# Transposing the attention probabilities by block moves and VectorE, a new order of the loop, and a new start of the kernel

## The chip, the cores and the metric

The kernel runs on one core of one Trainium2 chip. The metric is the device time of one execution in microseconds (us), the median of several executions of the whole program, with inputs and outputs in the chip's main memory.

## The reference

The input x has 8 sequences of 1024 rows of 512 numbers. An attention layer with a memory, and then a feed-forward layer, each followed by a residual sum and a layer norm:

```
q, k, v = x @ Wq, x @ Wk, x @ Wv            # 8 heads of 64, in segments of 128 rows
per head and segment, in order of segments:
    sq, sk  = elu(q) + 1, elu(k) + 1
    att_mem = sq @ mem / (sq @ z)
    mem, z  = mem + sk^T @ v, z + sum(sk)
    att_dot = softmax(q @ k^T / 8) @ v
    att     = gate * att_mem + (1 - gate) * att_dot      # gate = sigmoid(betas)
x = layernorm(x + concat(att) @ Wo)
W1q, W2q = each weight as -1, 0 or 1, after division by the mean of |W|
x = layernorm(x + relu(x @ W1q^T + b1) @ W2q^T + b2)     # 512 -> 2048 -> 512
```

Everything is float32.

## The kernel before

The program is written engine by engine, and every engine runs its own list, held in step by semaphores. The work is cut into 32 groups of two sequences by one segment (2 x 128 rows); two groups are live in the memory `mem`, so a group reads what the group two before it wrote. The main loop of each engine runs over g and does in iteration g a piece of group g (attention), of group g-1 and of group g-2 (feed-forward), in an order written out by hand.

Float32 products are made of float16 halves: an operand is split into a high half (ScalarE writes it) and a low half (VectorE or GpSimd subtracts), and TensorE adds three products (two where the weight is -1, 0 or 1). TensorE needs its operands with the summed index on the partitions, so x, the attention result, the normed rows and the probabilities have to be transposed. Three of these (`x_blocks`, `att_dot`, `y_blocks`), and `sk_t`, go by **moved blocks**: SyncE issues 16 DMAs (8 for x) that carry 32x32 blocks to their transposed places in runs of 128 bytes, and a VectorE instruction then turns each block where it lies. The probabilities go by TensorE: `turn_p` (L289) multiplies each 128x128 matrix by an identity, 16 matrices per group, into a PSUM bank, from which ScalarE (`p_split`, L1059) and VectorE (`p_split`, L660) write `pt_hi` and `pt_lo`.

TensorE's jobs of attention take turns in four PSUM banks (`take`, L214), each waiting until the bank's last reader is done. `ffn_up` (L366, eight pieces of a group, j = 0 to 7, 16 matmuls each) uses two banks more: piece j waits for the relu of piece j-2 (`h_relu`, L1086, ScalarE). `ffn_down` (L383, four pieces for each of the two sequences, 8 matmuls each) has a bank for each sequence, and needs the halves of h from `h_split` (VectorE, L771; pieces with an even j also their low half) and `h_rest` (GpSimd, L1303; the low half of those with an odd j). In iteration g, TensorE runs pieces 5 to 7 of `ffn_up` and all of `ffn_down` for group g-2, and pieces 0 to 4 of `ffn_up` for group g-1.

SyncE's list in an iteration is: blocks of x for g+1, `bounce_out` (the row maxima of x to main memory, from where `bounce_back` reads them to all partitions to find the scale of x), `move_y(g-1)`, `bounce_back`, `move_sk(g)`, `put_out(g-2)` (L1492), `move_att(g)`, and rows of x for g+2. A queue issues in order, so a step that waits holds what stands behind it. `load_x` (L1385) waits for the output that lay in the same rows.

Iteration 0 also prepares the weights: `w_max`, `w_split` and so on for the four attention weights, and for W1 and W2 the sums (`w_sum`), thresholds, 32 blocks of comparisons (`compare`, by VectorE and GpSimd), their transposes (`turn_w`) and copies (`put_w`). The gates' 512 values are spread to all partitions through main memory (`gates_out`, `gates_back`, L1434), in runs of 16 bytes. GpSimd multiplies by them in `gate_mix` (L1234).

The order in which `prob` comes to the matmuls:

```
def turn_p(g, t, half):                     # TensorE, bank from take()
    pe.wait_ge(sem["pexp"], by_half(g, t, half))
    for i in range(4):
        ins = pe.transpose(ps[:, i], prob[:, t, 4 * half + i], ident32[:])
```

Of the kernel before, what the change touches and what calls it, by code (L numbers as in the profile page):

```python
# [5 lines left out]
ALU = mybir.AluOpType  # L6
ACT = mybir.ActivationFunctionType
F32 = mybir.dt.float32
# [23 lines left out]
    xblocks ablocks yblocks skblocks xturn xt_hi xt kproj qproj kq_exp klo qlo elu vproj v_hi v1 v  # L32
    score rowmax exp_bias pexp pturn pt_hi pt skturn
    reset_fill reset mem num den attm invsum mix pv attd gated mixed upd
# [5 lines left out]
def build_program(nc, x, Wq, Wk, Wv, betas, Wo, W1, b1, W2, b2, out):  # L40
# [14 lines left out]
    with ctx:  # L55
# [33 lines left out]
        y_blocks = sb("y_blocks", [P, TG, D])  # L89
# [14 lines left out]
        pt_hi = sb("pt_hi", [P, TG, H, P], F16)  # L104
        pt_lo = sb("pt_lo", [P, TG, H, P], F16)
# [4 lines left out]
        at = sb("at", [P, TG, 2 * KT, P], F16)  # L110
# [10 lines left out]
        gate_dram = nc.dram_tensor("gate_dram", [P, 3, D // P], F32, kind="Internal").ap()  # L121
# [9 lines left out]
        h32 = flat[:, 4096:4096 + NH32 * 512].rearrange("p (b t) -> p b t", b=NH32)  # L131
        yt = sb("yt", [P, 2, TG, 2 * KT, P], F16)
# [42 lines left out]

        def two_pairs(rows_of, j):
            return rows_of[:, :, 2 * j:2 * j + 2].rearrange("p t c n -> p t (c n)")
# [28 lines left out]

        block = ctx.enter_context(nc.Block())

        @block.tensor
        def _(pe):  # L210
# [3 lines left out]
            def take(job):  # L214
# [6 lines left out]
                return b  # L221

# [32 lines left out]
            def project_v(g, t):  # L255
# [3 lines left out]
                if g == 0:  # L259
                    pe.wait_ge(sem["wsplit_pool"], 2)  # L260
# [27 lines left out]

            def turn_p(g, t, half):  # L289
                if not 0 <= g < NG:  # L290
                    return
                b = take(("p", g, t, half))
                ps = banks[b][:].rearrange("p (h t) -> p h t", h=4)
                pe.wait_ge(sem["pexp"], by_half(g, t, half))
                for i in range(4):
                    ins = pe.transpose(ps[:, i], prob[:, t, 4 * half + i], ident32[:])  # L296
                ins.then_inc(sem["pturn"], 1)
                bank_free[b] = (sem["pt"], by_half(g, t, half))
# [53 lines left out]
            def project_out(g, t):  # L352
# [3 lines left out]
                if g == 0 and t == 0:  # L356
                    pe.wait_ge(sem["wsplit_pool"], 4)
# [89 lines left out]
            spread_amax()  # L447
            turn_max(0)
            spread_max(0)
            for g in range(NG + 2):  # L450
                project_qk(g, "k", 0)
                if g == 0:
                    turn_max(1)
                    spread_max(1)
                    turn_max(2)
                    spread_max(2)
                ffn_up(g - 2, 5)
                project_qk(g, "k", 1)
                project_qk(g, "q", 0)
                ffn_up(g - 2, 6)  # L460
                project_qk(g, "q", 1)
# [1094 lines left out]
```

## Time and profile before

| what | value |
|---|---|
| median of 3 runs | 1965.37 us (1965.0 to 1965.46) |
| the profiled execution's own time | 1962.89 us |
| its span | 1961.1 us |
| granted TensorE clock, mean over the span | 0.982 of full speed |
| TensorE, matmuls busy | 1862.8 us |
| VectorE busy | 1488.7 us |
| ScalarE busy | 1003.6 us |
| GpSimd busy | 813.9 us |
| DMA | 619144 packets, 121.20 MB, of them 592800 packets under 512 B |

The span is the time from the first to the last instruction of the profiled execution; its own time is 1.79 us longer, and the median of the runs 2.48 us longer than that. An engine's busy time counts its instructions and not the issue of DMAs: what ScalarE's or SyncE's queue spends on those stands in the timeline of the queue. A matmul's record is longer than what the next one waits for; the distance between starts is the price of one.

### The profile page before, as it was taken

Reading aid. Unit: us, or ns where it says so; the run is one execution under the profiler, and the core shown is the slowest. Engines: PE = TensorE matmul, PEld = TensorE weight load, DVE = VectorE, ACT = ScalarE, POOL = GpSimd, SP = SyncE. Lnnn points to the kernel's source line nnn. Section 1 sums busy time; section 2 is a strip of 40 time slices with the busy share of each in tenths; the row PEclk is TensorE's granted clock in tenths of the full one; section 3 lists DMA queues with packets and bytes.
Section 4 is the critical chain, followed back from the end, with each engine's and each line's share of the span. In section 5 each row is a group of like instructions: output and inputs, shape, how many; then the busy total and the mean of one; then the engine's idle time right before and its main releaser. Section 6 shows DMA issues by size and latency. Waiting matters only on the chain.

```text
span 1961.1 us, 44984 instructions
## 1 busy us (share of the span) xinstructions
PE 1862.8 (95%) x16663; PEld 1312.6 (67%) x16663; DVE 1488.7 (76%) x2991; ACT 1003.6 (51%) x2426; POOL 813.9 (42%) x810
## 2 busy tenths in 40 slices
PE   3478999999999999999999999999999999999987
PEld 2266666777766677776667777666677776667754
DVE  4577877777887777778877777887777788777763
ACT  2655555455555555554555555455545555555531
POOL 0563443344444334444443444444334444433443
PEclk9688999999999999999999999999999999999999
DMA  7932233333323333332323233223332332323121
GB/s 226 105 74 50 47 55 57 60 59 65 64 45 61 53 58 61 63 67 45 60 52 63 58 60 67 54 53 56 57 59 58 66 63 47 61 50 62 37 39 33
DMA packets 619144, 121.20 MB, mean 62 GB/s; under 512 B 592800, under 2 KB 596784, under 8 KB 618416
## 3 DMA queue, kind: packets, MB, share of 16 engines
q1 hardware_dynamic: 616640, 114.11, 30.9%
q10 hardware_dynamic: 2288, 4.20, 0.6%
q8 instruction: 135, 2.21, 0.5%
q14 instruction: 81, 0.66, 0.2%
HBM read 51.06 MB, written 16.80 MB: 35 GB/s over the span
## 4 chain that ended last, share of the span: by engine, by line
PE 91%; DVE 3%; issue 2%; SPq 2%; ACT 1%; POOL 1%; DMA 0%; POOLq 0%; DVEq 0%; ACTq 0%
PE bank L393 11%; PE bank L379 11%; PE bank L380 11%; PE bank L394 11%; PE bank L249 6%; PE bank L251 6%; PE bank L250 6%; PE bank L317 3%; PE bank L263 3%; PE bank L296 3%; PE bank L360 3%; PE bank L265 3%; PE bank L361 3%; PE bank L264 3%; PE bank L362 3%
## 5 line engine op out<-in xcount | busy, mean ns | idle before, releaser
L379 PE MATMUL bank<-yt,w1t 128*128 128x256 f16 x2048 | 456.9, 273 | 2.9 <-POOL yt L1278 2.9
L380 PE MATMUL bank<-yt,w1t 128*128 128x256 f16 x2048 | 456.5, 273 | 0.0
L1101 ACT ACTIVATE arena<-bank,b_scaled,wscalars 128x256 f32<-128x256 f32 x512 | 261.4, 562 | 379.4 <-PE bank L380 291.5
L393 PE MATMUL bank<-w2t,arena 128*128 128x512 f16 x1024 | 388.7, 380 | 2.1 <-POOL arena L1310 2.1
L394 PE MATMUL bank<-w2t,arena 128*128 128x512 f16 x1024 | 388.1, 379 | 0.0
L1055 ACT ACTIVATE prob<-bank,exp_bias,gscalars 128x128 f32<-128x128 f32 x512 | 227.2, 459 | 229.8 <-DVE exp_bias L657 228.6
L1310 POOL TENSOR_TENSOR arena<-arena 128x512 f16<-128x512 f32 x128 | 172.0, 1344 | 270.3 <-DVE arena L780 270.3
L1271 POOL TENSOR_TENSOR at<-att_dot,at 128x512 f16<-128x512 f32 x64 | 74.1, 1159 | 416.7 <-ACT at L1074 416.7
L379 PEld LDWEIGHTS bank<-yt,w1t 128*128 128x128 f16 x2048 | 200.7, 98 | 28.4 <-issue 3.4
L380 PEld LDWEIGHTS bank<-yt,w1t 128*128 128x128 f16 x2048 | 200.7, 98 | 22.6
L393 PEld LDWEIGHTS bank<-w2t,arena 128*128 128x128 f16 x1024 | 100.0, 98 | 113.6 <-issue 3.1
L1243 POOL TENSOR_TENSOR att_mem<-att_mem,gate_in 128x512 f32<-128x512 f32 x64 | 81.7, 1276 | 220.3 <-DVE att_mem L696 197.1
L394 PEld LDWEIGHTS bank<-w2t,arena 128*128 128x128 f16 x1024 | 100.2, 98 | 106.7
L620 DVE SCALAR_TENSOR_TENSOR k_lo<-bank,k_hi 128x512 f16<-128x512 f32 x64 | 44.2, 691 | 139.2 <-ACT relu_tmp L1028 139.2
L249 PE MATMUL bank<-xt,wk_hi 128*128 128x256 f16 x512 | 141.1, 276 | 6.3 <-DVE wk_lo L812 6.0
L780 DVE CAST arena<-arena 128x512 f16<-128x512 f32 x256 | 139.0, 553 | 7.7 <-ACT arena L1101 7.5
L783 DVE TENSOR_TENSOR arena<-arena 128x512 f16<-128x512 f32 x128 | 140.4, 1097 | 4.4
L250 PE MATMUL bank<-xt,wk_hi 128*128 128x256 f16 x512 | 141.0, 275 | 0.0
L251 PE MATMUL bank<-xt,wk_lo 128*128 128x256 f16 x512 | 141.0, 275 | 0.0
L251 PE MATMUL bank<-xt,wq_lo 128*128 128x256 f16 x512 | 139.6, 273 | 0.0
L249 PE MATMUL bank<-xt,wq_hi 128*128 128x256 f16 x512 | 139.6, 273 | 0.0
L250 PE MATMUL bank<-xt,wq_hi 128*128 128x256 f16 x512 | 139.6, 273 | 0.0
(177 smaller groups left out, 4464.2 us busy)
## 6 DMA issues: line engine op xcount, KB each, us to landing
x_blocks<-in_L_attn_x SPq DMA_DIRECT2D x256, 64.0 KB, 2.9
rows<-in_L_attn_x SPq DMA_DIRECT2D x32, 512.0 KB, 3.9
sk<-sk_t SPq DMA_DIRECT2D x512, 32.0 KB, 2.0
att_dot<-att_mem SPq DMA_DIRECT2D x512, 32.0 KB, 2.0
y_blocks<-rows SPq DMA_DIRECT2D x512, 32.0 KB
out_rows<-rows SPq DMA_DIRECT2D x64, 256.0 KB, 2.0
arena<-in_L_ffn_W SPq DMA_DIRECT2D x6, 1024.0 KB, 5.8
w2t<-in_L_ffn_W SPq DMA_DIRECT2D x2, 1024.0 KB, 9.6
```

What stands on the lines that cost most here:

```text
L249: pe.matmul(ps[:, :, c], w_hi[n][:, k, cols], xt[:, :, k], start=k == 0, stop=False)
L250: pe.matmul(ps[:, :, c], w_hi[n][:, k, cols], xt[:, :, KT + k], start=False, stop=False)
L251: ins = pe.matmul(ps[:, :, c], w_lo[n][:, k, cols], xt[:, :, k], start=False, stop=k == KT - 1)
L379: pe.matmul(ps[:, c], w1t[:, k, cols], yt[:, g % 2, :, k], start=k == 0, stop=False)
L380: ins = pe.matmul(ps[:, c], w1t[:, k, cols], yt[:, g % 2, :, KT + k], start=False, stop=k == KT - 1)
L393: pe.matmul(banks[own][:], h_hi[:, f, toks], w2t[:, f, :], start=f == 0, stop=False)
L394: ins = pe.matmul(banks[own][:], h_lo[:, f, toks], w2t[:, f, :], start=False, stop=f == FT - 1)
L780: dve.tensor_copy(hi, h32[:, n % NH32]).then_inc(sem["h_hi"], 1)
L783: dve.tensor_tensor(lo, h32[:, n % NH32], hi, ALU.subtract).then_inc(sem["h_dve"], 1)
L1055: ins = act.activation(prob[:, t, at], ps[:, c], ACT.Exp, scale=gcol(g, G_EXP), bias=exp_bias[:, t, at:at + 1], accum_out=row_sum[:, t, h: ...
L1101: ins = act.activation(h32[:, n % NH32, c * GT:(c + 1) * GT], ps[:, c], ACT.Relu, scale=w(H_SCALE_Y), bias=b1_scaled[:, f:f + 1])
L1310: pool.tensor_tensor(lo, h32[:, n % NH32], hi, ALU.subtract).then_inc(sem["h_pool"], 1)
```

## The change

1. **The probabilities.** TensorE's `turn_p` goes. Once all exponentials of a group are there, ScalarE's queue issues 16 DMAs (`move_p`) of 64 KB, that carry 32x32 blocks of `prob` to `p_blocks`; VectorE turns the blocks (two instructions of 128x1024 per group), and the two `p_split` read `p_blocks` in SBUF in place of PSUM banks. `pt_hi` and `pt_lo` now lie over `prob`, so the exponentials of a group wait for `pv` of the group before.
2. **The order of the loop.** All engines' lists are written anew. The whole feed-forward of a group (eight pieces up, eight down) is now in one iteration, g-2; `update_memory` is done one iteration later. On SyncE `bounce_back` follows `bounce_out` at once, `move_att(g)` stands before `put_out(g-2)`, and `load_x` right behind that.
3. **The start.** Group 0 is not loaded as blocks: its rows are the first DMA, the maximum is taken of them, and TensorE transposes them (8 transposes). All weight loads go through SyncE, k, q, v first. Low halves of Wv are VectorE's in place of GpSimd's. The gates are written to main memory so that they are read back in runs of 2 KB.

The core of the diff (the engines' loops are shown for TensorE; the others are rewritten in the same way):

```diff
+        def move_blocks(engine, dst, src, done):
+
+            for b in range(4):
+                for a in range(4):
+                    engine.dma_start(dst[32 * a:32 * a + 32, :, :, 32 * b:32 * b + 32],
+                                     src[32 * b:32 * b + 32, :, :, 32 * a:32 * a + 32]).then_inc(done, 16)
...
-                    act.wait_ge(sem["pturn"], by_half(g - 1, t, half))
+                    act.wait_ge(sem["pv"], by_t(g - 1, t))
...
+            def move_p(g):
+                act.wait_ge(sem["pexp"], by_half(g, 1, 1))
+                if g:
+                    act.wait_ge(sem["pt"], by_half(g - 1, 1, 1))
+                move_blocks(act, p_blocks, prob, sem["pblocks"])
...
+            def turn_p(g, t):
+                flat_p = p_blocks[:, t].rearrange("p h c -> p (h c)")
+                dve.wait_ge(sem["pblocks"], MOVED * (g + 1))
+                dve.transpose(flat_p, flat_p).then_inc(sem["pturn"], 1)
...
-                pool.wait_ge(sem["gated"], 2 * by_t(g, t))
+                pool.wait_ge(sem["gated_in"], by_t(g, t))
+                pool.wait_ge(sem["gated"], by_t(g, t))
...
-                    sp.dma_start(gate[:].rearrange("p (n q) -> p n q", q=D // P),
-                                 gate_dram[:, i].partition_broadcast(P)).then_inc(sem["gates"], 16)
+                    sp.dma_start(gate[:], gate_dram[i].rearrange("p n -> (p n)").partition_broadcast(P)).then_inc(sem["gates"], 16)
```

TensorE's list of an iteration, without what only g = 0 has. Before:

```
k 0 | up(g-2,5) | k 1, q 0 | up(g-2,6) | q 1 | up(g-2,7) | out(g-1, 0 and 1) | scores 0 | v 0
| down(g-2, 0: 0, 1) | turn_p | v 1 | down(g-2, 0: 2) | scores 1 | read 0 | down(g-2, 0: 3; 1: 0) | turn_p
| down(g-2, 1: 1) | turn_p x2 | attend 0 | down(g-2, 1: 2) | read 1 | down(g-2, 1: 3) | attend 1
| up(g-1, 0 to 3) | update(g, 0 and 1) | up(g-1, 4)
```

After:

```
k 0, k 1, q 0, q 1 | up(g-2, 0, 1) | update(g-1, 0) | read 0 | scores 0 | up(g-2, 2, 3) | scores 1
| update(g-1, 1) | up(g-2, 4) | out(g-1, 0 and 1) | up(g-2, 5) | v 0 | read 1 | up(g-2, 6)
| down(g-2, 0: 0) | v 1 | up(g-2, 7) | down(g-2, 0: 1, 2, 3; 1: 0) | attend 0 | down(g-2, 1: 1)
| attend 1 | down(g-2, 1: 2, 3)
```

**ScalarE, a middle group, from the exponentials to the split of the probabilities.** The tile `arena` holds h (the relu of `ffn_up`). Before:

```order
L1055 ACTIVATE prob,row_sum<-bank,exp_bias,gscalars 128x128 x4
L1041 ACTIVATE v_hi<-bank 128x512
L1042 ACTIVATE v<-bank,gscalars 128x8x64
L1055 ACTIVATE prob,row_sum<-bank,exp_bias,gscalars 128x128 x4
L1066 ACTIVATE pt_hi<-bank 128x512
L1041 ACTIVATE v_hi<-bank 128x512
L1042 ACTIVATE v<-bank,gscalars 128x8x64
L1055 ACTIVATE prob,row_sum<-bank,exp_bias,gscalars 128x128 x8
L1066 ACTIVATE pt_hi<-bank 128x512 x2
```

With the change:

```order
L1080 ACTIVATE prob,row_sum<-bank,exp_bias,gscalars 128x128 x4
L1132 ACTIVATE arena<-bank,b_scaled,wscalars 128x256 x2
L1080 ACTIVATE prob,row_sum<-bank,exp_bias,gscalars 128x128 x4
L1132 ACTIVATE arena<-bank,b_scaled,wscalars 128x256 x2
L1080 ACTIVATE prob,row_sum<-bank,exp_bias,gscalars 128x128 x8
L1132 ACTIVATE arena<-bank,b_scaled,wscalars 128x256 x2
L217 DMA p_blocks<-prob 32x16x32 x16
L1132 ACTIVATE arena<-bank,b_scaled,wscalars 128x256 x4
L1066 ACTIVATE v_hi<-bank 128x512
L1067 ACTIVATE v<-bank,gscalars 128x8x64
L1132 ACTIVATE arena<-bank,b_scaled,wscalars 128x256 x2
L1097 ACTIVATE prob<-p_blocks 128x512 x4
```

The relus of pieces 2, 3 and 4 now stand between the exponentials, and those of pieces 5, 6 and 7, the split of v and all four `p_split` stand behind the 16 DMAs.

**SyncE, one iteration in the middle of the program.** Before:

```order
L1408 DMA x_blocks<-in_L_attn_x 32x16x32 x8
L1449 DMA amax_dram<-amax 128x1
L1464 DMA y_blocks<-rows 32x8x32 x16
L1456 DMA amax_row<-amax_dram 128x128
L1476 DMA sk<-sk_t 32x8x32 x16
L1497 DMA out_rows<-rows 128x512 x2
L1464 DMA att_dot<-att_mem 32x8x32 x16
L1395 DMA rows<-in_L_attn_x 128x2x512
```

With the change:

```order
L1430 DMA x_blocks<-in_L_attn_x 32x16x32 x8
L1473 DMA amax_dram<-amax 128x1
L1480 DMA amax_row<-amax_dram 128x128
L217 DMA y_blocks<-rows 32x8x32 x16
L217 DMA sk<-sk_t 32x8x32 x16
L217 DMA att_dot<-att_mem 32x8x32 x16
L1509 DMA out_rows<-rows 128x512 x2
L1417 DMA rows<-in_L_attn_x 128x2x512
```

The read back of the maxima stands right behind their write, ahead of the blocks of y, and the output right ahead of the load into the rows it frees.

## Rows read from the trace of the kernel before

**Rows 1.** The page: busy time of each engine, and the chain that ended last
```profile
PE 1862.8 (95%) x16663; PEld 1312.6 (67%) x16663; DVE 1488.7 (76%) x2991; ACT 1003.6 (51%) x2426; POOL 813.9 (42%) x810
...
PE 91%; DVE 3%; issue 2%; SPq 2%; ACT 1%; POOL 1%; DMA 0%; POOLq 0%; DVEq 0%; ACTq 0%
```

**Rows 2.** Timeline of VectorE, the turn of sk in groups 2, 15 and 31: start us, us
```profile
215.79 1.23 DVE L635 STREAM_TRANSPOSE sk_t<-sk_t 128x1024 f32<-128x1024 f32 x1
...
953.75 1.24 DVE L635 STREAM_TRANSPOSE sk_t<-sk_t 128x1024 f32<-128x1024 f32 x1
...
1861.42 1.24 DVE L635 STREAM_TRANSPOSE sk_t<-sk_t 128x1024 f32<-128x1024 f32 x1
```

**Rows 3.** Timeline of TensorE, ends of groups 14 and 15's passes: start us, us
```profile
907.36 0.38 PE L394 MATMUL bank<-w2t,arena 128*128 128x512 f16 x1
907.58 1.04 PE L296 MATMUL bank<-ident,prob 128*128 128x128 f32 x8
908.45 0.19 PE L331 MATMUL bank<-v_hi,pt_hi 128*128 128x64 f16 x1
...
924.26 0.27 PE L380 MATMUL bank<-yt,w1t 128*128 128x256 f16 x1
924.37 0.27 PE L249 MATMUL bank<-xt,wk_hi 128*128 128x256 f16 x1
```

**Rows 4.** Groups of instructions by line: x count, busy us, mean ns, idle before
```profile
L296 PE MATMUL bank<-ident,prob 128*128 128x128 f32 x512 | 74.6, 280 | 7.7 <-ACT prob L1055 7.7
...
L635 DVE STREAM_TRANSPOSE sk_t<-sk_t 128x1024 f32<-128x1024 f32 x32 | 39.5, 1233 | 0.0
...
L666 DVE SCALAR_TENSOR_TENSOR pt_lo<-bank,pt_hi 128x512 f16<-128x512 f32 x128 | 87.8, 686 | 30.3 <-ACT pt_hi L1066 30.3
...
L607 DVE SCALAR_TENSOR_TENSOR xt<-x_blocks,gscalars,xt 128x512 f16<-128x512 f32 x64 | 47.7, 747 | 27.4 <-ACT xt L1010 27.4
```

**Rows 5.** Timeline of ScalarE: a relu pair, and half a group's exponentials
```profile
933.25 1.03 ACT L1101 ACTIVATE arena<-bank,b_scaled,wscalars 128x256 f32<-128x256 f32 x2
934.24 0.60 ACT L1022 ACTIVATE q_hi<-bank 128x512 f16<-128x512 f32 x1
...
948.34 0.46 ACT L1055 ACTIVATE prob<-bank,exp_bias,gscalars 128x128 f32<-128x128 f32 x1 [3.61 <-DVE exp_bias L657]
...
950.09 0.60 ACT L1041 ACTIVATE v_hi<-bank 128x512 f16<-128x512 f32 x1
```

**Rows 6.** Timeline of SyncE's queue in one group: start us, us, DMAs issued
```profile
665.32 10.42 SPq L1464 DMA_DIRECT2D y_blocks<-rows  x16
...
676.48 10.89 SPq L1476 DMA_DIRECT2D sk<-sk_t  x16
...
692.56 11.03 SPq L1464 DMA_DIRECT2D att_dot<-att_mem  x16
...
704.27 5.61 SPq L1408 DMA_DIRECT2D x_blocks<-in_L_attn_x  x8
```

**Rows 7.** The page's DMA issues: xcount, KB each, median us to landing
```profile
x_blocks<-in_L_attn_x SPq DMA_DIRECT2D x256, 64.0 KB, 2.9
...
amax_dram<-amax SPq DMA_DIRECT2D x31, 0.5 KB, 7.2
```

**Rows 8.** Chain of waits at the start, in order of time: start us, us
```profile
3.08 0.71 SPq L1408
...
3.83 3.12 SPq L1408
...
17.41 1.23 DVE amax L536
...
31.09 0.40 PE bank L249
...
135.58 0.27 PE bank L249
```

**Rows 9.** Timeline of GpSimd in group 0: the gates' wait
```profile
96.03 1.26 POOL L1243 TENSOR_TENSOR att_mem<-att_mem,gate_in 128x512 f32<-128x512 f32 x1 [23.27 <-DMA gate_out<-gate_dram]
```

More of the change, by code:

```diff
@@ L221, in take, with turn_x @@
                 return b
+            def turn_x(t):
+                b = take(("x", t))
+                ps = banks[b][:].rearrange("p (k c) -> p k c", k=KT)
+                pe.wait_ge(sem["ident"], 1)
+                pe.wait_ge(s_x[0], 16)
+                for k in range(KT):
+                    ins = pe.transpose(ps[:, k], rows[:, 0, t, k * P:(k + 1) * P], ident32[:])
+                ins.then_inc(sem["xturn"], 1)
+                bank_free[b] = (sem["xt"], t + 1)
             def turn_w(n):
@@ L287, in scores @@
                 ins.then_inc(sem["score"], 1)
[L289 to L298, printed above, removed]
             def read_memory(g, t):
@@ L447, in _ @@
             spread_amax()
+            turn_x(0)
+            turn_x(1)
             turn_max(0)
@@ L461, in _ @@
                 project_qk(g, "q", 1)
+                ffn_up(g - 2, 0)
+                ffn_up(g - 2, 1)
+                update_memory(g - 1, 0)
+                read_memory(g, 0)
+                scores(g, 0)
+                ffn_up(g - 2, 2)
+                ffn_up(g - 2, 3)
+                scores(g, 1)
+                update_memory(g - 1, 1)
                 if g == 0:
                     turn_max(3)
-                ffn_up(g - 2, 7)
+                    spread_max(3)
+                ffn_up(g - 2, 4)
@@ L476, in _ @@
+                ffn_up(g - 2, 6)
                 ffn_down(g - 2, 0, 0)
-                ffn_down(g - 2, 0, 1)
-                turn_p(g, 0, 0)
-                project_v(g, 1)
-                ffn_down(g - 2, 0, 2)
                 if g == 0:
                     sum_all(1)
-                scores(g, 1)
-                read_memory(g, 0)
+                project_v(g, 1)
+                ffn_up(g - 2, 7)
+                ffn_down(g - 2, 0, 1)
+                if g == 0:
+                    sum_all(2)
+                    for n in range(0, 4):
+                        turn_w(n)
+                    for n in range(4, 8):
+                        turn_w(n)
@@ L499, in _ @@
                     for n in range(8, 12):
                         turn_w(n)
-                ffn_down(g - 2, 1, 2)
-                read_memory(g, 1)
-                ffn_down(g - 2, 1, 3)
-                attend(g, 1)
-                ffn_up(g - 1, 0)
-                if g == 0:
                     for n in range(12, 16):
                         turn_w(n)
-                ffn_up(g - 1, 1)
-                ffn_up(g - 1, 2)
-                ffn_up(g - 1, 3)
-                update_memory(g, 0)
+                ffn_down(g - 2, 1, 1)
@@ L515, in _ @@
                         turn_w(n)
-                update_memory(g, 1)
+                attend(g, 1)
                 if g == 0:
@@ L521, in _ @@
                         turn_w(n)
+                ffn_down(g - 2, 1, 2)
+                ffn_down(g - 2, 1, 3)
+                if g == 0:
                     for n in range(28, 32):
                         turn_w(n)
-                ffn_up(g - 1, 4)
         @block.vector
@@ L945, in _ @@
                         compare(n)
-                residual(g - 2, 0, 1)
-                p_split(g, 0, 1)
+                v_split(g, 0)
+                x_scale(g + 1, 1)
+                scale_sums(g, 1)
+                h_split(g - 2, 7)
+                x_scale(g + 1, 2)
+                x_scale(g + 1, 3)
+                turn_p(g, 0)
+                turn_p(g, 1)
+                if g == 0:
+                    threshold(2)
+                p_split(g, 0, 0)
                 if g == 0:
```

385 lines of the change are left out of this document (182 added, 203 removed).

## The prediction

> **What bounds the kernel now.** I read the page's busy shares and its chain first [rows 1]: TensorE is busy in 95% of the span and holds 91% of the chain that ended last. Then the length of a group. The turn of `sk` stands at 215.79, 953.75 and 1861.42 in groups 2, 15 and 31 [rows 2]: 29 intervals of 56.75 us. Between starts, a 512-column matmul costs 0.22 us and a 256-column one 0.11 [rows 3], and TensorE's list adds up to about 56.3, so it runs nearly without a gap. The span is then three parts. The first projection of group 15 is at 924.37 [rows 3], 29.4 ahead of its turn; taken back to group 2 that gives 186.4 for the start, 30 iterations of 56.75, and 72.2 for the end. VectorE, ScalarE and GpSimd have slack [rows 1]. SyncE is nearer its limit: y, sk and att take 10.4, 10.9 and 11.0, the blocks of x 5.6 [rows 6], 38 us of 56.75 in block moves alone.
>
> **The sum, a middle iteration.** *TensorE loses the transposes*: eight take 0.87 us from start to next start [rows 3], 16 a group 1.74, so 56 us over 32 groups. The floor of an iteration is 55.0. (The busy time of the group, 74.6, is not the price, since records overlap [rows 4].) Everything else is added elsewhere.
>
> *ScalarE's queue gets 16 DMA issues.* No row shows one of 64 KB between tiles of this memory. SyncE's of 32 KB take 10.42 for 16, 0.65 each, and those of 64 KB from main memory 5.61 for 8, 0.70 each [rows 6]; so 10.4 from below and 11.2 from the form that has as many runs of 128 bytes. The upper end is 1.3 each, 20.8, if two issuing queues share one issuer. I take 11.2, by the row of the same size. Does it fit? With t = 0 at the first k projection, the q projections end at 10.5 (96 x 0.109). ScalarE splits q until 12.4, has two relus and two `at_hi`, and the score of sequence 0 comes at 16.2; the maximum and the bias give the first exponential at 17.6. A half's exponentials take 1.75 and a relu pair 0.97 [rows 5], so four halves and three relus end at 27.5, the issues at 38.7, and relu 5 at 39.7. Piece 7 of `ffn_up` needs that relu's bank. Ahead of it TensorE has four projections 10.5, seven pieces up 12.2, one down 1.7, out and v 10.4, scores, reads and updates 4.4: it arrives at 39.3. So it waits **0.4 us an iteration**, and every us that the issues take more is a us of wait. Behind it, relu 7 ends at about 42.8, its low half on GpSimd at 44.6, where `ffn_down` piece 3 comes at 44.9: no further wait.
>
> The rule that speaks for a smaller price: the Trainium skill, "DMA: Bandwidth & Descriptors", section "Issuing engines are not separate DMA queues", says that issuing from several engines saves only the sequencer's time, which is usually small against the DMA. By it the 11.2 would be near nothing and the sum 12 us lower; the issue rows speak against it here.
>
> *The probabilities' way.* Issued at 38.7, landed about 3 later (2.9 for the 64 KB form [rows 7]), at 41.6. VectorE turns two times 1024 columns at 1.23 [rows 4] behind its part of relu 7: until 45.7. Four `p_split` of each engine follow, the last low half at about 49. `attend` for sequence 0 comes at 48.4 and needs only the first two, done at 48; for sequence 1 at 50.9. Cost nothing, with half a microsecond to spare; without this cover it is paid one for one.
>
> *VectorE* gets 2.5 for the turns and reads two SBUF operands in `p_split`: 0.75 in place of 0.69 by the row of `xt` [rows 4], 0.2 a group. It goes from 76% busy to 47.7 of 55.4 us, 86%, and waits about 4 us for relu 5 ahead of the turns, so I cost it at nothing. It is next to be late.
>
> *SyncE* keeps its issues but its waits change. The write of the maxima takes 7.2 to land [rows 7], under which y's moves were issued; now nothing is, so the queue stands for it. Output then load adds 2 for the output's landing. From att's start: att 11.0, output and landing 2.5, rows 0.6, x blocks 4.9 and 2.9 to land, maximum 1.2, bounce 7.2 and 0.6, y 10.4, sk 10.9: 52.3, against 55.0. So it fits with under 3 us of slack.
>
> An iteration is then 55.4.
>
> **The sum, start and end.** At the start the maximum waited for blocks of x until 17.41, behind issues as long as 3.12, and the first projection came 13.7 later, at 31.09 [rows 8]. Rows as the first DMA should be there at about 5.5, and VectorE's turns of x (1.3) go: first projection near 18. In group 0 GpSimd waited 23.3 for the gates at 96.03 [rows 9], with comparisons queued behind it and the next group starting at 135.58 [rows 8]. With runs of 2 KB, and five comparisons ahead of the gates, most of that goes. Against it, the 11.2 of issues now stand ahead of three of the eight weight sums on which the transposes of weights wait. I take 13 and 10.5 off: group 1 at 112. Iteration 1 has no feed-forward work now and took 50.8; SyncE's cycle lets it take 48. Group 2 starts at **160** (bounds 150 and 180) instead of 186.4. The end gets work that iteration 1 lost: pieces 0 to 4 up of group 30 (8.7) and `update_memory` (1.1), so 72.2 becomes about **81** (bounds 77 and 88).
>
> 160 + 30 x 55.4 + 81 = 1903. The profiled execution's time is 1.8 above its span and the median 2.5 above that, so **1907**. The middle gives 40, the start 26, the end costs 9.
>
> **The rivals.**
>
> *The issues on ScalarE's queue cost more: slower, or the same.* The place is `ffn_up` piece 7, the price 30 us on the program for each us over 11.2. It turns at 13.1, or 0.82 an issue: then an iteration is 57.3 and the sum 1961. It speaks for it that SyncE issues y from about 33.6, inside the move from 27.5 to 38.7, that both go to the same DMA engines, and that an issue of SyncE's took 3.12 when the engines were full [rows 8]. Against it: one just ahead took 0.71 while ScalarE's queue was issuing too, and a middle group's DMA load is far from full. If the five us that overlap go at half speed, the issues take 15.3, an iteration 59.5, and the time is 2030; in the middle of the two ends, 1995. Chance 0.19. The Trainium skill, "VectorE: DVE Perf Modes", section "Rules for kernel authors", says to transpose 128x128 on TensorE where a PSUM destination will do, which is the kernel before; this rival is how it would be right.
>
> *SyncE's cycle becomes the bound.* With 52.3 at hand, four or five us of contention or of late VectorE ahead of the maximum give 56.2 to 57.4 an iteration: 1931 to 1967. Late att blocks would hold VectorE at the turn of `att`, ahead of the score maxima. For it: a second queue runs beside it. Against it: the moves of y and sk are at their shortest in the row though matmuls and loads run. Chance 0.14, two thirds of it faster.
>
> *The start gives nothing back.* If the sums behind the 11.2 of issues hold the weights' transposes as long as the gates did, group 2 starts at 186 and the time is 1933. Chance 0.10.
>
> **How the numbers follow.** The forecast has 0.57, with its own range 1885 to 1945 (150 or 180 for the start, 55.0 or 56.0 for an iteration). A measurement of this kernel tells 0.2%, 4 us, from no change. Faster is the forecast, the start's rival and two thirds of SyncE's: 0.76. Slower is the first rival and a little of SyncE's: 0.21; the rest, 0.03, is the same. The range goes from 1885 up to 1975, which takes in SyncE's rival and the near end of the first, and leaves out 0.16.
>
> **What would show it.** No matmul reads `prob` with the identity, and TensorE's list is shorter by 1.74 a group. The turn of `sk` comes at a distance of 55.0 to 56.0; TensorE's only repeated wait is at `ffn_up` for a relu of ScalarE's, under 1 us. The 16 issues take 10.4 to 12 in ScalarE's queue, and SyncE waits some 7 us between write and read of the maxima. The second group's first projection stands at about 112, and GpSimd's wait for gates is a few us. I am wrong if TensorE waits several us for ScalarE or for the blocks, if an issue takes over 0.8, or if SyncE has no wait left in its cycle.

## The result, and the profile after

The change is **slower**: 2112.65 us (median of 4 runs, 2108.36 to 2113.74) against 1965.18 for the kernel before, a ratio of 1.0749 with a 95% interval of 1.073 to 1.0768. I had forecast 1907, with a range from 1885 to 1975, and the time lies outside it. The profiled execution took 2113.74 us, 1.8 over its span.

The page of the change, its busy times and its chain, to set beside [rows 1]; "ACTq" is ScalarE's queue while it issues DMAs:

```profile
span 2111.9 us, 44385 instructions
...
PE 1887.2 (89%) x16159; PEld 1291.3 (61%) x16159; DVE 1583.3 (75%) x3055; ACT 995.6 (47%) x2426; POOL 806.9 (38%) x806
...
PE 29%; ACTq 21%; ACT 20%; DVE 19%; issue 10%; POOL 1%; DMA 0%; DVEq 0%; POOLq 0%
```

TensorE held 91% of the chain and now holds 29%. No engine has a larger share of the span than it had; the chain now runs through ScalarE's queue, ScalarE and VectorE in turn. That is a loop of waits, not a full engine.

The distances between first k projections, from group 2 to group 31 (29 of them), have a mean of 62.0 us; before they were 56.77 each. In parts:

| part | predicted | measured |
|---|---|---|
| start, to group 2 | 160 | 170.2 |
| 29 iterations | 55.4 each | 62.0 each |
| the next one, without a write of maxima | 55.4 | 58.2 |
| end | 81 | 85.5 |
| span | 1903 | 2111.9 |

So 191 of the 209 us over the sum are the 29 iterations. Where do they wait? The waits of the whole execution: what waited, on what, us in total, times, longest.

```profile
ACT arena L1132 <- issue: 428.7, 30, 16.8
...
PEld bank L395 <- ACT arena L1132: 102.9, 40, 6.7
PE bank L395 <- ACT arena L1132: 86.2, 29, 6.2
ACT exp_tmp L1052 <- DVE sk_t L644: 69.7, 61, 1.4
...
PE bank L333 <- DVE sq_t L644: 50.9, 32, 4.1
```

L1132 is the relu, L395 `ffn_up`, L333 the read of the memory. ScalarE's relu 5 stands 14 us an iteration behind "issue", its own queue; TensorE waits for it at piece 7; and a second, smaller wait is at the read, for `sq_t`. One move (iteration from 1038.05) on ScalarE's and on SyncE's queue, and TensorE at piece 7:

```profile
1067.30 0.61 ACTq L217 DMA_DIRECT2D p_blocks<-prob  x1
...
1067.94 14.45 ACTq L217 DMA_DIRECT2D p_blocks<-prob  x15
1082.50 1.93 ACT L1132 ACTIVATE arena<-bank,b_scaled,wscalars 128x256 f32<-128x256 f32 x4 [14.31 <-issue]
```

```profile
1067.87 0.33 SPq L1473 DMA_DIRECT2D amax_dram<-amax  x1
1076.33 0.33 SPq L1480 DMA_DIRECT2D amax_row<-amax_dram  x1
```

```profile
1079.50 0.38 PE L292 MATMUL bank<-wv_hi,xt 128*128 128x512 f16 x1
1083.57 0.28 PE L395 MATMUL bank<-yt,w1t 128*128 128x256 f16 x1 [3.70 <-ACT arena L1132]
1083.69 0.27 PE L396 MATMUL bank<-yt,w1t 128*128 128x256 f16 x1
...
1084.66 0.42 PE L396 MATMUL bank<-yt,w1t 128*128 128x256 f16 x1
1084.87 0.42 PE L395 MATMUL bank<-yt,w1t 128*128 128x256 f16 x1
```

The 16 issues take 15.1 us here, from the start of the first to the end of the last (15.07 in the mean of groups 2 to 31), where my sum had 11.2. They overlap a write of the maxima of x to main memory: 128 runs of 4 bytes, issued 0.57 us behind the first issue and waited for by SyncE until 1076.33. In group 31, the only one of these with no such write beside its move, the move takes 11.1. The excess is not spread over the issues. In each of the moves 1 to 30 one to three issues take 1 us or more, the longest between 2.0 and 7.0, and the median of all issues is 0.66 us (min/median/max in ns, of the change):

```profile
L217 ACTq DMA_DIRECT2D p_blocks<-prob x512: 592/656/6982, 52.6 to 2008.0; - x171
```

Behind the wait, TensorE's starts soon lie 0.21 apart in place of 0.11: it runs at the lower of its two clock levels (1.2 in place of 2.4 GHz) for the rest of piece 7 and two matmuls behind it. The 16 matmuls of the piece take 3.0 us from first start to next start, 1.3 more than at 0.11, and the two behind it 0.4 more.

The second wait, 1.46 us for `sq_t` at 1054.27 and so 29 us earlier in the same iteration, begins here. VectorE and GpSimd in the splits of k:

```profile
1042.72 0.69 DVE L637 SCALAR_TENSOR_TENSOR k_lo<-bank,k_hi 128x512 f16<-128x512 f32 x1 [0.21 <-ACT relu_tmp L1053]
1043.33 1.66 DVE L644 SCALAR_TENSOR_TENSOR sk_t<-exp_tmp,relu_tmp 128x512 f32<-128x512 f32 x1
...
1046.99 1.66 DVE L644 SCALAR_TENSOR_TENSOR sk_t<-exp_tmp,relu_tmp 128x512 f32<-128x512 f32 x1
...
1050.64 0.68 DVE L644 SCALAR_TENSOR_TENSOR sq_t<-exp_tmp,relu_tmp 128x512 f32<-128x512 f32 x1
```

```profile
1043.28 1.16 POOL L1302 TENSOR_TENSOR yt<-y_blocks,yt 128x512 f16<-128x512 f32 x1 [2.14 <-ACT yt L1115]
1046.94 1.16 POOL L1302 TENSOR_TENSOR yt<-y_blocks,yt 128x512 f16<-128x512 f32 x1 [2.50 <-ACT yt L1115]
```

The same VectorE form takes 1.66 us where GpSimd's subtraction of two tiles lies beside it, and 0.68 where nothing does. Twice a group, and ScalarE waits for each, so the exponentials come at t = 20.3 in place of my 17.6.

**Theory A**: ScalarE's issues, lengthened by the write of the maxima, hold relu 5 and so piece 7. **Theory B**: `sk_t` beside GpSimd, and the late q and k that follow. **Theory C**: SyncE's cycle, or VectorE's load, is the bound. **Theory D**: the new order costs by itself, by something else than B.

### The profile page after: what moved, and what is told of

The parts are those of the page before. It is cut to its first block, busy times and chain, and to the rows that moved or that the text cites. A ratio compares the mean times of both kernels' runs of the same rounds, so it can differ in the third digit from the quotient of the medians.

```text
span 2111.9 us, 44385 instructions
## 1 busy us (share of the span) xinstructions
PE 1887.2 (89%) x16159; PEld 1291.3 (61%) x16159; DVE 1583.3 (75%) x3055; ACT 995.6 (47%) x2426; POOL 806.9 (38%) x806
## 4 chain that ended last, share of the span: by engine, by line
PE 29%; ACTq 21%; ACT 20%; DVE 19%; issue 10%; POOL 1%; DMA 0%; DVEq 0%; POOLq 0%
ACTq L217 21%; ACT prob L1080 10%; PE bank L409 7%; PE bank L410 7%; DVE sk_t L644 5%; ACT arena L1132 4%; ACT relu_tmp L1053 4%; PE bank L395 3%; PE bank L396 3%; ACT exp_tmp L1052 2%; DVE sq_t L644 2%; DVE rows L772 2%; DVE stats L776 2%; PE bank L333 2%; DVE xt L624 2%
## 5 line engine op out<-in xcount | busy, mean ns | idle before, releaser
L395 PE MATMUL bank<-yt,w1t 128*128 128x256 f16 x2048 | 504.3, 290 | 99.5 <-ACT arena L1132 86.2
L396 PE MATMUL bank<-yt,w1t 128*128 128x256 f16 x2048 | 502.8, 289 | 0.0
L1132 ACT ACTIVATE arena<-bank,b_scaled,wscalars 128x256 f32<-128x256 f32 x512 | 258.8, 583 | 483.2 <-issue 428.7
L409 PE MATMUL bank<-w2t,arena 128*128 128x512 f16 x1024 | 393.8, 385 | 0.0
L410 PE MATMUL bank<-w2t,arena 128*128 128x512 f16 x1024 | 392.4, 383 | 0.0
L803 DVE CAST arena<-arena 128x512 f16<-128x512 f32 x256 | 156.1, 610 | 230.2 <-ACT arena L1132 229.4
L395 PEld LDWEIGHTS bank<-yt,w1t 128*128 128x128 f16 x2048 | 212.1, 104 | 160.8 <-ACT arena L1132 102.9
L1334 POOL TENSOR_TENSOR arena<-arena 128x512 f16<-128x512 f32 x128 | 148.7, 1162 | 389.7 <-DVE arena L803 389.7
L396 PEld LDWEIGHTS bank<-yt,w1t 128*128 128x128 f16 x2048 | 212.1, 104 | 36.5
L1269 POOL TENSOR_TENSOR att_dot<-att_dot,gate_out 128x512 f32<-128x512 f32 x64 | 107.7, 1683 | 186.8 <-DVE att_dot L731 186.8
L1047 ACT ACTIVATE k_hi<-bank 128x512 f16<-128x512 f32 x64 | 38.2, 597 | 276.8 <-PE bank L278 276.8
L1052 ACT ACTIVATE exp_tmp<-bank,gscalars 128x512 f32<-128x512 f32 x128 | 87.8, 686 | 100.0 <-DVE sk_t L644 69.7
```

What stands on the lines that cost most here:

```text
L395: pe.matmul(ps[:, c], w1t[:, k, cols], yt[:, g % 2, :, k], start=k == 0, stop=False)
L396: ins = pe.matmul(ps[:, c], w1t[:, k, cols], yt[:, g % 2, :, KT + k], start=False, stop=k == KT - 1)
L409: pe.matmul(banks[own][:], h_hi[:, f, toks], w2t[:, f, :], start=f == 0, stop=False)
L410: ins = pe.matmul(banks[own][:], h_lo[:, f, toks], w2t[:, f, :], start=False, stop=f == FT - 1)
L803: dve.tensor_copy(hi, h32[:, n % NH32]).then_inc(sem["h_hi"], 1)
L1132: ins = act.activation(h32[:, n % NH32, c * GT:(c + 1) * GT], ps[:, c], ACT.Relu, scale=w(H_SCALE_Y), bias=b1_scaled[:, f:f + 1])
```

## The experiments

The kernel before ran beside each set of runs, with a median of 1963 to 1965. "An iteration" is the mean of the 29 distances. One time of one run has no interval; the effects asked for are 10 to 70 us, and the kernel before spreads over 3 or 4. The length of a move is always taken from the start of its first issue to the end of its last; where an expectation of a later run says 11.4 for a move, the traces have 11.7 by this measure, and where it says 57.9 or 58.2 for an iteration, the mean is 58.1.

### Fewer moves, or none

```diff
-                move_blocks(act, p_blocks, prob, sem["pblocks"])
+                move_blocks(act, p_blocks, prob, sem["pblocks"], range(2))
```

> ScalarE issues 8 of the 16 DMAs that carry the probabilities (the rest of p_blocks stays zero, so the outputs lack half of the attention scores' part). Theory A (ScalarE's queue: the issues hold relu 5 and with it ffn_up piece 7): the issues fall from 15.1 to about 7.5 us, so the wait of 4 us ahead of piece 7 and the slow clock behind it (1.2 us) go; an iteration takes about 57 in place of 62, the time is 1950 to 1970. Theory B (late q and k halves, VectorE slowed beside GpSimd): the 4 us are paid elsewhere, the iteration stays within 1 us of 61 to 62, 2080 to 2110. Theory C (SyncE's cycle): y's issues are only a little quicker, 2080 to 2110.

> No DMA of the probabilities at all; VectorE turns and both engines split a p_blocks that holds zeros, so the attention scores' part of the result is left out. Theory A: like the half, 1940 to 1965; an iteration of 56 to 57 (floor 55.0 plus the 1.5 us that the first score halves are late). Theory B or C: 2080 to 2110, as nothing of theirs goes. If half_moves and no_moves agree, half of the issues already fitted under TensorE's work.

Measured: 1987.71 with half of the moves, 1990.61 with none; 58.1 and 58.2 an iteration. Both are far below the 2080 of B and C, which fall as sole causes, and both are above A's ranges, by 18 and 26 us, so A is not the whole. The moves are worth 3.8 us an iteration, and there is nothing to gain below half of them.

The short write stayed in both kernels. With half of the moves it lay beside the move in every group from 1 to 30, and yet in 16 of them the eight issues took their undisturbed 5.4 us; in the other 14 one to three issues took longer, and the move took 5.5 to 11.1. One of the 16, with the write issued in its midst and waited for until 1070.63:

```profile
1061.06 4.75 ACTq L217 DMA_DIRECT2D p_blocks<-prob  x7
```

```profile
1061.36 0.34 SPq L1474 DMA_DIRECT2D amax_dram<-amax  x1
```

So a write on its way does not slow every issue; it makes single ones long. What remains in 58.2 is 2.8 us over my 55.4. The windows of one iteration of the kernel without moves (us, TensorE busy, clock, DMA share, GB/s):

```profile
868.60:873.00 4.40, 4.40 (x48) 1.00 0.34 65
873.00:876.00 3.00, 1.54 (x32) 0.93 0.48 160
876.00:880.00 4.00, 4.00 (x44) 0.62 0.90 209
880.00:916.80 36.80, 36.80 (x297) 1.00 0.20 33
```

TensorE stands still for 1.46 us at 873.4 (the wait for `sq_t`), and then runs at 0.62 of its clock for 4 us. In 4 of the 28 iterations from group 3 on the same wait left the clock at its full level, and these took 56.9 us in place of 58.2 to 58.5: the clock costs 1.4. The wait and the clock behind it are the 2.8.

### The write of the maxima left out, and kept as one run

```diff
-                sp.dma_start(amax_dram[g], amax[:, g % 2]).then_inc(s_there[g % 2], 16)
+                sp.dma_start(amax_dram[g:g + 1], ones_all[0:1, :]).then_inc(s_there[g % 2], 16)
```

The edit shown is the second one's: the write keeps its place, size and target, but comes from one partition and carries a constant; the floor of x's scale is set so that the scale stays the same power of two. In the first kernel nothing is written, and the read fetches 128 values of x. In both, VectorE no longer waits for the write.

> The maxima of x are not written to main memory for groups 1 to 31; the read that follows reads 128 values of x, so the scale of x is another one, all else stays. It tests whether the write, whose 128 runs of 4 bytes are outstanding for 8 us, stretches ScalarE's issues. If so (part of theory A), a move takes 11.1 us as in group 31 in place of 15.1, an iteration about 58, the time 1985 to 2000. If the stretch is from y's issues or the other traffic, a move stays at 14 to 15 and the time within 15 us of 2112 minus what SyncE's cycle gives.

> The write of the maxima stays at its place in SyncE's list, of the same 512 bytes to the same place, but as one run of 512 bytes from one partition in place of 128 runs of 4 bytes; its value is a constant, and the floor of the scale is set so that the scale is the same power of two as before. Leaving the write out took an iteration from 62.0 to 58.2 us and a move of the probabilities from 15.1 to 11.4. Theory A1 (the 128 short runs hold up ScalarE's issues): as without the write, 1985 to 1992, moves of 11.2 to 12. Theory A2 (any write that SyncE waits for, or its landing, does it; or SyncE's y issues then start at a worse time): moves of 14 to 15 and 2095 to 2113.

Measured: 1987.84 without it, 1988.37 with it as one run; 58.1 an iteration in both, moves of 11.7 in the mean of both. The write as one run, at the same place:

```profile
1059.95 0.61 ACTq L217 DMA_DIRECT2D p_blocks<-prob  x1
1060.58 11.21 ACTq L217 DMA_DIRECT2D p_blocks<-prob  x15
```

```profile
1060.86 0.25 SPq L1473 DMA_DIRECT2D amax_dram<-ones_all  x1
1062.02 0.35 SPq L1480 DMA_DIRECT2D amax_row<-amax_dram  x1
```

512 bytes to the same place, 0.91 us behind the move's first issue: SyncE waits 1.2 us for it in place of 8.5, and ScalarE's move takes 11.8 in place of 15.1. The issues of this kernel, to set beside those of the change:

```profile
L217 ACTq DMA_DIRECT2D p_blocks<-prob x512: 592/655/1809, 52.1 to 1881.9; - x171
```

A2 falls: not a write, but a write of 128 runs of 4 bytes from 128 partitions lengthens the other queue's issues. The Trainium skill, "DMA: Bandwidth & Descriptors", section "Specifications", puts the smallest transfer at full rate at 512 bytes and has smaller ones read and written back; this agrees with the order of the two. The price to another queue is what these runs show.

The two kernels without moves and without the short write agree within 3 us, so a move of 11.7 us costs next to nothing on the path, as my sum had it: TensorE waits for a relu at `ffn_up` ten times in all in one_run_write, 6.0 us together. What a move takes above that is paid.

### GpSimd's subtraction replaced by a fill

```diff
-                pool.tensor_tensor(yt[:, g % 2, t, KT:2 * KT], in_cols(y_blocks, t), yt[:, g % 2, t, 0:KT],
-                                   ALU.subtract).then_inc(sem["yt"], 1)
+                pool.memset(yt[:, g % 2, t, KT:2 * KT], 0.0).then_inc(sem["yt"], 1)
```

> GpSimd writes zeros as the low half of y in place of the subtraction of two tiles (so the first feed-forward product lacks its low half). In the change this subtraction runs beside VectorE's sk_t and sq_t, which take 1.67 us in place of 0.69, and the scores come 2.8 us later than I predicted. Theory B (GpSimd's reads slow VectorE there): sk_t falls to about 0.7, the exponentials and with them the move and relu 5 come 2 to 3 us earlier, and the wait of 1.5 ahead of the first read goes: 2 to 4 us an iteration, 1990 to 2055. Rival (VectorE's two-operand form is slow here by itself, or the write alone disturbs it): no change, 2095 to 2113.

Measured: 2073.32, 60.7 an iteration. `sk_t` of the change, and of this kernel (x count, busy us, mean ns):

```profile
L644 DVE SCALAR_TENSOR_TENSOR sk_t<-exp_tmp,relu_tmp 128x512 f32<-128x512 f32 x64 | 102.1, 1596 | 0.0
```

```profile
L644 DVE SCALAR_TENSOR_TENSOR sk_t<-exp_tmp,relu_tmp 128x512 f32<-128x512 f32 x64 | 43.6, 681 | 0.0
```

The mechanism of B is shown: 1596 ns falls to 681, and TensorE's wait for `sq_t` from 50.9 us to 7.1. GpSimd still writes there (a fill of 0.53 us), and in part at the same time as `sk_t`, so it is its reading that VectorE waits for. `sq_t`, which my expectation also called slow, was at 681 ns in the change already. The time falls by 39 us, 1.3 an iteration, which is less than the 2 to 4 that I expected and outside my range, because TensorE reaches piece 7 earlier too: its wait for relu 5 grows from 86.2 to 114.8. The Trainium skill, "SBUF — State Buffer", section "Who interferes with whom", says that a VectorE instruction with two inputs in this memory contends with a GpSimd instruction that reads there, not with one that only writes, and calls the port pair that they share an exclusive lock. The rows agree: 1.16 us of GpSimd, 0.98 added to `sk_t`, nothing added beside a fill. So does the trace of before, where `pt_lo`, with one input in a bank, overlaps the same subtraction by over 0.3 us 33 times and stays at 0.68.

`sk_t` was not the only one. In the change `xt` takes 1.40 us in place of 0.74 in about half of its instructions, each time with both products of the gates beside it, and its mean goes from 747 ns to 1051. It stays so in the kernel of the next section, so it is no part of what is found there.

### Both causes away

one_run_write with the fill above, nothing else. It leaves out what these two do: the low half of y, and a scale of x taken from x.

> Both causes taken away at once: the write of the maxima as one run of 512 bytes, and GpSimd's subtraction for the low half of y replaced by a fill with zeros (that low half is left out of the product). one_run_write alone gave 57.9 an iteration, y_low_fill alone took sk_t from 1.60 to 0.68 us and the wait for sq_t from 50.9 to 7.1 us in all. Theory A plus B (these two are the whole of what my sum lacks): an iteration of 55.3 to 56.0 and 1905 to 1930, which is my prediction. Rival (a third cause, such as VectorE's 86% or SyncE's cycle, holds it): 57 to 58, 1960 to 1985.

Measured: **1912.56**, 55.6 an iteration, group 2 at 159.3. My prediction was 1907, with 55.4 and 160. The page, and what is left of TensorE's waits:

```profile
PE 1819.3 (95%) x16159; PEld 1259.9 (66%) x16159; DVE 1514.9 (79%) x3055; ACT 1003.9 (53%) x2426; POOL 766.9 (40%) x806
...
PE 72%; ACTq 9%; ACT 9%; DVE 4%; issue 2%; SPq 2%; POOL 1%; DMA 1%; DVEq 0%; POOLq 0%
```

So the two causes are the whole of what the iterations lack: 62.0, less 3.9 for the write, less 2.5 for GpSimd. In the other order it is 1.3 for GpSimd and then 5.1 for the write, since TensorE, once one wait is gone, comes earlier to the other. Theory C falls: in an iteration of 55.6 VectorE is busy 45.9 us, or 83%, and SyncE's cycle fits in.

### The order alone

Moves and VectorE's turns away, TensorE's `turn_p` back, on the new order and the new start; v's second split comes ahead of the splits of the probabilities.

> Undo of the probabilities' part alone: TensorE turns them again (two of its sets in ahead of ffn_down pieces), both engines split from PSUM, no moves and no VectorE turns; the new order and the new start stay, except that v's second split stands ahead of relu 7. Theory A (the moves' issues are the cost, and the new order itself costs only the wait at the first read): with no moves at all an iteration was 58.2, plus 1.74 of transposes is 59.9, the time 2035 to 2050, slower than the 1965 of before. Rival (the order is as good as the old one, and the 58.2 comes from VectorE's turns of p): an iteration of 56.8, 1945 to 1960.

> The last kernel of this kind put a turn between the two v projections, so that the second projection waited 4.2 us an iteration for a bank that v's split held, which is my edit's and not the order's. Here the turns come behind piece 7 of ffn_up, and v's splits as early as in the change. No moves, TensorE turns, the new order and start. Theory A: 58.2 without moves plus 1.74 of transposes, an iteration of 59.9 to 60.5: 2035 to 2055. Rival (the order itself is as good as the old one, 56.8): 1945 to 1960.

The first gave 2200.14: its `turn_p` between the two v projections changed which bank the second one gets, and TensorE waited for `v_lo`:

```profile
PE bank L290 <- DVE v_lo L675: 135.7, 32, 9.3
```

The second gave 2023.49 and 59.4 an iteration, a little below the expected range. So the order, with the turns where I put them, costs 2.6 us against the 56.77 of before: it puts y's subtraction beside `sk_t` (1580 ns here) and the read right behind the splits (49.9 us of waits for `sq_t`). That is about the 2.5 us of B, so little is left for theory D. The probabilities' part, once the short write is one run, gains 1.3 against this (58.1), of 1.74 for the transposes.

### TensorE's list put in another order

Four kernels try to step around the waits. All but up7_later also let TensorE turn and spread the maxima (two small matmuls), so that nothing is written in the loop.

> A candidate to beat both: the change with two edits. TensorE turns the maxima's column and spreads the maximum for every group (two small matmuls in bank 7), so nothing goes through main memory; and TensorE's read of the memory for sequence 0 stands behind scores 0 and ffn_up piece 2 in place of ahead of scores 0, so that it does not wait for sq_t. The first edit should give what no_maxima_write gave (58.2 an iteration), the second take away the wait of 1.46 us and the stretch at the half clock behind it (1.4): 55.4 to 56.0 an iteration. With 167 for the start and 84 for the end: 1915 to 1935. Rival (the first exponentials, not the read, hold relu 5, and up 7 then waits for it): 57 to 58, 1960 to 1990.

> The change with the maxima turned and spread by TensorE (no write to main memory), and piece 2 of ffn_up ahead of the read of sequence 0, which fills the wait of 1.46 us for sq_t. In read_later the read stood between the two scores, and TensorE waited 3 us an iteration for the exponentials, since the four banks then come round in another order; here the order of the banks stays. Without the write an iteration was 58.2. Theory A: the wait and the half clock behind it go, and relu 5 (t = 42) is now later than piece 7 (t = 39.8): 56.5 to 57.5, the time 1935 to 1965. Rival (VectorE or the score's chain keeps the 58.2): 1980 to 1992.

> The change as it is, with its write of the maxima and its moves of 15 us, but piece 7 of ffn_up comes two pieces of ffn_down (3.5 us) later in TensorE's list, and VectorE turns the probabilities ahead of its half of relu 7. Theory A (the long queue on ScalarE costs only through relu 5 ahead of piece 7): the 4 us of wait shrink to 0.5 to 1 and the clock dip behind them goes, an iteration of 58.2 to 59.2: 1988 to 2020, although a move still takes 14 to 17 us. Rival (the late landing of the probabilities holds attend as well): the wait moves to attend, 2070 to 2110.

> A candidate against both: up2_first, with piece 7 of ffn_up two pieces of ffn_down later, VectorE's turns of p ahead of its half of relu 7, and in group 0 the first projection ahead of the turns of q's maximum. Theory A: no wait for relu 5, none for sq_t, an iteration of 55.2 to 56.2 against a floor of 55.0; first projection at 15, group 2 at 155 to 160, the end 84: 1895 to 1930. Rival (the probabilities, at 50 to 51, are late for attend): 57 to 58, 1950 to 1985.

| kernel | time | iteration | TensorE now waits |
|---|---|---|---|
| read_later | 2076.83, ratio 1.0571 (1.0554 to 1.0589) | 61.0 | 93.7 us for exponentials, at scores 1 |
| up2_first | 2018.33 | 59.1 | 50.7 for `att_mem`, at scores 1 |
| up7_later | 2152.8 | 63.3 | 93.5 for GpSimd's low half of relu 7 |
| candidate | 2066.05, ratio 1.0524 (1.0507 to 1.0542) | 60.6 | 50.9 for `att_mem`, 37.1 for `yt` |

```profile
PE bank L309 <- ACT prob L1086: 93.7, 32, 5.8
```

```profile
PE bank L409 <- POOL arena L1334: 93.5, 29, 5.7
```

All four missed, and were above the rivals' ranges too, by two faults of mine. L309 waits for a bank, not for its operands: the jobs take four banks in turn, so a job that is moved changes whose reader the later ones wait for, and a read that comes later frees its banks later. And in up7_later the wait was there because data are late: relus 6 and 7 and v's split stand behind the long queue as relu 5 does, so TensorE only met the next of them, through GpSimd. The rival of that run had the right kind of thing at the wrong place.

### The start alone, on the old loop

> The loop of the kernel before with the start of the change alone: rows of group 0 first, its maximum from the rows, TensorE turns them, all weight loads on SyncE, gates read in runs of 2 KB. The start of the change gained 16 us up to group 2 with half of it in the first projection (31.1 to 20.1) and the rest by the gates. Theory that the start is a gain by itself: 1940 to 1952. Rival, that the gates' wait is only moved to the transposes of weights, as in group 0 of the change (98 us against 104): 1952 to 1958.

Measured: **1935.24** (1934.35 to 1936.99), ratio 0.9855 (0.9838 to 0.9873): faster than both kernels. First projection at 14.65, group 1 at 106.2, group 2 at 157.2, then 56.77 an iteration as before. The gain of 30 us is beyond what I expected of it. In the change the first projection comes at 20.1, since two turns and spreads of the weights' maxima are ahead of it in TensorE's list; in the kernels of the next section, which put it ahead of these, it comes at 14.8 and 14.7.

### A whole kernel without both causes

TensorE turns and spreads the maxima; the turn and both splits of y stand at the end of the iteration before; the first projection of group 0 is ahead of the maxima of q.

> A whole kernel without both causes: TensorE turns and spreads the maxima (nothing written to main memory in the loop), and the turn and the split of y for sequence 0 and 1 stand at the end of the iteration before on VectorE, ScalarE and GpSimd, away from the splits of q and k; and in group 0 the first projection is ahead of the turns of q's maximum. If the causes are these two: 55.5 to 56.5 an iteration, first projection at 15, group 2 at 155 to 160, the end 84: 1905 to 1940. Rival (y's work at the end delays xt or attend's halves by as much): 57 to 58.5, 1950 to 1990.

> In y_earlier sk_t was back at 0.68 us, but ScalarE waited 5 us an iteration (318.8 in all) for VectorE's turn of y, which I had put behind the normalisation, so that the split of k began 2.6 us late. Here VectorE turns both sequences of y ahead of the residual, GpSimd's two subtractions stand between its two small jobs, and the last normalisation of a group comes behind k's first split in the next iteration. If the two causes are all: an iteration of 55.3 to 56.5, group 2 at 157, the end 84: 1900 to 1935, so below the 1935.2 of front_only. Rival (VectorE's list, at 86% busy, has no free place for y there, so k's split stays late): 57.5 to 58.5, 1965 to 1995.

y_earlier gave 2009.87 (ratio 1.0232, 1.0215 to 1.0249) and 58.9 an iteration, above both of its ranges: `sk_t` was at 681 ns, but ScalarE waited for VectorE's turn of y ahead of k's split:

```profile
ACT yt L1120 <- DVE y_blocks L797: 318.8, 64, 13.5
```

y_earlier_2 puts VectorE's turns ahead of the residual and the last normalisation behind k's split:

```diff
+                turn_y(g - 1, 0)
+                turn_y(g - 1, 1)
                 residual(g - 2, 0, 1)
                 residual(g - 2, 1, 1)
                 scalars(g + 1, 0)
-                turn_y(g - 1, 0)
...
-                turn_y(g - 1, 1)
-                normalise(g - 2, 1, 1)
...
                 qk_split(g, "k", 0)
+                normalise(g - 3, 1, 1)
```

Measured: **1924.46** (1920.46 to 1926.55), ratio 0.9795 (0.9778 to 0.9812), 56.0 an iteration. It beats both kernels and front_only, and it leaves nothing out.

```profile
PE 1833.7 (95%) x16252; PEld 1269.9 (66%) x16252; DVE 1523.1 (79%) x3055; ACT 1013.3 (53%) x2426; POOL 806.0 (42%) x806
...
PE 69%; ACT 8%; ACTq 8%; DVE 5%; SPq 4%; issue 3%; POOL 2%; DMA 1%; DVEq 0%; POOLq 0%
```

## Why the prediction was wrong

**What bounds the kernel before, and the floor of 55.0.** Right. With both causes away TensorE is busy 95% again and an iteration is 55.6; 13 of the 29 take 55.1.

**The 16 issues at 11.2 us.** This is the term that failed, by its size: 15.07 in the mean. The form and its price were nearly right (11.7 in the mean without the short write), and so was what hangs on it: at 11.7 it costs next to nothing, and 3.4 us more cost 3.9. That is over the one us for each us of my sum, which had no term for the lower clock level behind a wait. It was the first rival, at 0.19, and its time of 2030 is about what the term alone would have given (30 times 3.9 over 1907 is 2024). That its 15.3 lies beside the measured 15.1 is luck: five us at half speed add five, which is 16.2 and not 15.3, and the rival named the wrong neighbour, y's issues on SyncE. In the change these start some 9 us into the move, in 23 of the moves 1 to 30 the longest issue is over before the first of them, and in one_run_write, where y's issues overlap the move's end too, it takes 11.7. A hint lay in the trace of before: y's moves there begin with a write of the maxima on its way, issued 5 to 6 us earlier, in all groups but the last two, and I took one of the shortest [rows 6]. The 30 of them take 10.39 to 14.35, again with one or two long issues where they are long, and the two without a write take 10.38. Two of the long ones:

```profile
892.73 13.56 SPq L1464 DMA_DIRECT2D y_blocks<-rows  x16
...
949.15 13.74 SPq L1464 DMA_DIRECT2D y_blocks<-rows  x16
```

I did see that the change puts nothing on SyncE's queue under the write's 7.2 us, and priced that for SyncE, but not that ScalarE's move would now lie on it whole. That the write is the cause in this trace too was not tried.

**The time line to the first exponential, t = 17.6.** Wrong by 2.7 us, and the second term. I took each split of q and k at its undisturbed length; the new order lets y's subtraction run beside `sk_t`. The cost beside the first cause is 1.3 us an iteration, and 2.5 once that is gone, about half of it the clock level behind the wait. The trace of before had this too. Of its 64 `sq_t` 32 lie beside GpSimd's subtraction for `at` and take 1.66 us, so that the mean stands between the two lengths, while `sk_t` is at 681:

```profile
L627 DVE SCALAR_TENSOR_TENSOR sq_t<-exp_tmp,relu_tmp 128x512 f32<-128x512 f32 x64 | 74.7, 1167 | 0.0
```

**VectorE at nothing.** Right as far as its load goes; wrong in that I weighed only its own two-input form and not what GpSimd does beside it. The form itself costs nothing more: `p_split` takes 0.675 us from this memory, where I had 0.75, and 0.686 from a bank before.

**SyncE's cycle of 52.3, under 55.** Right: with the write as one run an iteration of 55.6 is reached. That run also shortened the cycle by 7 us. With the write as it was the shortest iteration is 56.6, in half_moves, and below that the cycle is not tried.

**The probabilities' way.** Right: in one_run_write and one_run_y_fill, with moves of 11.7 and 11.8, TensorE waits for a split of the probabilities once in all, for 7.0 us.

**The start, 160.** 170.2. Without the short write it was 158.0 to 159.1: the term was right but for the same cause, which also lengthens the moves of groups 0 and 1. **The end, 81.** 85.5, and about 84 in the kernels without the causes, within my bounds; 72.2, 8.7 and 1.1 add up to 82 and not 81.

**That the middle would gain.** Of the change's three parts the start gives 30 us by itself, the order costs 2.6 us an iteration, and the probabilities' part gains 1.3 only when the write is no longer made of short runs.

## What to carry to other kernels

Before a queue of an engine that computes is given many DMAs, look at what else is on its way at that time, and take the price from the spread of such issues in the trace, not from the shortest. When an order is rewritten, lay the lists of VectorE and GpSimd beside each other: a group whose mean stands between two lengths of the same form shows a neighbour that holds it. And a wait for late data is not cured by other work put ahead of it; find what made the data late.

## What the runs showed of the hardware

A write of 512 bytes as 128 runs of 4 bytes, waited for 8.5 us beside a move, lengthened 16 issues on the other queue from 11.7 to 15.1 us; as one run it was there after 1.2 us, and the move took what it takes without a write. The time went into one to three issues of a move, of 1 to 7.0 us each, and eight issues beside the same write were undisturbed in 16 groups of 30. I had not expected one queue to pay for the other's form of a write. Why the issues wait, whether for a shared issuer or for room at the DMA engines, no run tells apart. In the change the DMA engines are busy 0.48 of the 100 us from 1000 on.

A VectorE instruction with both inputs in this memory took 1.66 us in place of 0.68 beside a GpSimd subtraction of 1.16 us, and was undisturbed by a GpSimd fill. After a stop of TensorE of 1.5 or 4 us the next microseconds ran at the lower clock level (0.62 in the window of 4 us), in most iterations but not in all. Without moves the distance was 58.2 to 58.5 in 24 of 28 iterations, and 56.9 in the four where the level held, so the level cost 1.4 us where it fell; behind the stop of 3.7 us that is shown above it was 1.7.
